# Cross attention: keys turned by a product with a rounded identity, and VectorE takes most copies of turned keys and queries

## The reference, cut to what matters

```python
q = x @ Wq.T + bq                      # 512 x 256, 16 heads of 16
kv = c @ Wkv.T + bkv                   # 1601 x (keys, values)
q = _rms_norm(q, q_gamma)
k = _rms_norm(k, k_gamma)
scores = jnp.einsum('bhnd,bhmd->bhnm', q, k) * scale
attn = jax.nn.softmax(scores, axis=-1)
out = jnp.einsum('bhnm,bhmd->bhnd', attn, v)
```

## Time and profile before

| | us |
|---|---|
| median of 3 runs | 1317.8 |
| lowest and highest | 1315.87, 1321.56 |
| profiled execution, device time | 1319.82 |
| its span, first to last instruction | 1318.1 |
| PE busy | 1209.0 (92%) |
| ACT busy | 907.4 (69%) |
| POOL busy | 706.0 (54%) |
| DVE busy | 659.2 (50%) |

### The profile page before, as it was taken

The page is one execution under the profiler, slowest core; times in us unless marked ns, Lnnn a source line. Parts: engine busy times, 40 slices in busy tenths (PEclk is TensorE's granted clock), DMA queues, the critical chain, the costliest instruction groups (busy, mean ns, idle before and its releaser), DMA issues.

```text
span 1318.1 us, 27754 instructions
## 1 busy us (share of the span) xinstructions
PE 1209.0 (92%) x8712; PEld 739.7 (56%) x8712; DVE 659.2 (50%) x2198; ACT 907.4 (69%) x1824; POOL 706.0 (54%) x810
## 2 busy tenths in 40 slices
PE   5999999999999885799999999999999989999897
PEld 4667766776677573433334333433333278888794
DVE  6666567557655556555035502552555163333336
ACT  4656556646645615667986798679998848888892
POOL 1776557656756701445415540564267757765552
PEclk9999999999999998899999999999999999999999
DMA  7998665445445721001001100101056386666677
GB/s 236 361 318 274 240 206 189 170 153 188 172 149 192 239 64 35 26 13 31 17 1 51 33 17 2 51 2 35 29 208 227 115 302 197 200 219 195 193 270 301
DMA packets 146756, 195.05 MB, mean 148 GB/s; under 512 B 12049, under 2 KB 132513, under 8 KB 145969
## 3 DMA queue, kind: packets, MB, share of 16 engines
q1 hardware_dynamic: 135856, 162.97, 37.9%
q0 software_dynamic: 10752, 30.26, 6.2%
HBM read 71.01 MB, written 122.18 MB: 147 GB/s over the span
## 4 chain that ended last, share of the span: by engine, by line
PE 55%; ACT 16%; issue 10%; DVE 8%; DMA 5%; POOL 3%; SPq 2%; ACTq 0%; DVEq 0%; POOLq 0%
ACT xa_probs L1404 9%; PE sa_pf L354 8%; PE xa_banks L1243 7%; PE xa_banks L1258 6%; PE sa_po L436 5%; PE xa_banks L1126 5%; PE sa_pf L387 4%; PE sa_ps L411 4%; PE mo_banks L2172 4%; PE sa_ptr L422 4%; DMA mo_xs<-rows 3%; ACT sa_probs L478 2%; PE mo_banks L2181 2%; DMA mo_w_all<-in_down_p 1%; PE mo_banks L2160 1%
## 5 line engine op out<-in xcount | busy, mean ns | idle before, releaser
L1404 ACT ACTIVATE xa_probs<-xa_banks 128x1024 f32<-128x1024 f32 (+1 forms) x416 | 401.9, 1045 | 83.2 <-PE xa_banks L1243 82.3
L341 POOL TENSOR_SCALAR sa_probs<-sa_probs,sa_recip 128x128 f32<-128x128 f32 (+3 forms) x256 | 275.7, 1090 | 170.1 <-DVE sa_recip L598 169.6
L478 ACT ACTIVATE sa_probs<-sa_probs,sa_neg_max 128x128 f32<-128x128 f32 (+3 forms) x256 | 141.8, 555 | 155.4 <-DVE sa_neg_max L535 155.3
L1258 PE MATMUL xa_banks<-xa_probs,xa_v_one 128*17 128x512 f32 (+1 forms) x1664 | 218.7, 598 | 6.9 <-ACT xa_q_aug L1350 4.6
L1243 PE MATMUL xa_banks<-xa_q_aug,xa_k_aug 32*128 32x512 f32 (+1 forms) x1664 | 153.3, 442 | 13.5 <-issue 3.4
L2088 POOL DMA_INDIRECT slots<-mo_y,mo_dest x128 | 123.9, 968 | 69.5 <-issue 35.5
L2172 PE MATMUL mo_banks<-mo_xs_t,mo_gu 128*128 128x128 f32 x1024 | 136.3, 276 | 0.0
L2172 PEld LDWEIGHTS mo_banks<-mo_xs_t,mo_gu 128*128 128x128 f32 x1024 | 125.5, 193 | 0.4 <-issue 0.2
L535 DVE CUSTOM_DVE_ANT_0 sa_probs<-sa_ps,sa_toeplitz 128x128 f32<-128x128 f32 (+3 forms) x256 | 115.1, 486 | 14.9 <-PE sa_ps L411 13.4
L1243 PEld LDWEIGHTS xa_banks<-xa_q_aug,xa_k_aug 32*128 32x128 f32 (+1 forms) x1664 | 61.5, 179 | 106.2 <-ACT xa_probs L1404 74.5
L2232 ACT ACTIVATE mo_gu<-mo_w_all 128x512 f32 x128 | 80.7, 630 | 35.3 <-issue 15.3
(11 more groups left out here) (343 smaller groups left out, 2287.5 us busy)
## 6 DMA issues: line engine op xcount, KB each, us to landing
rows<-sa_blank SPq DMA_DIRECT2D x128, 548.0 KB, 3.8
mo_xs<-rows SPq DMA_DIRECT2D x106, 137.0 KB
slots<-sa_blank SPq DMA_DIRECT2D x48, 256.0 KB, 5.0
mo_w_all<-slots SPq DMA_DIRECT2D x22, 512.0 KB, 16.5
xa_raw<-in_ctx_t SPq DMA_DIRECT2D x24, 256.0 KB, 2.8
mo_w_all<-in_gate_up_p SPq DMA_DIRECT2D x2, 2816.0 KB, 16.1
sa_toeplitz<-extended_bias SPq DMA_DIRECT2D x8, 512.0 KB, 7.6
mo_w_all<-in_down_p SPq DMA_DIRECT2D x2, 2048.0 KB, 16.9
```

Of the source, the lines that this page charges most:

```text
L341: pool.tensor_scalar(probs[:, t % SLOTS, 0:w], probs[:, t % SLOTS, 0:w], recip[:, col:col + 1], None, ALU.mult).then_inc(probs_ready, 1)
L478: act.activation(probs[:, t % SLOTS, 0:w], probs[:, t % SLOTS, 0:w], ACT.Exp, bias=neg_max[:, i:i + 1], scale=-1.0, accum_out=sums[:, i:i ...
L1258: last = pe.matmul(banks[32 * i:32 * i + XD + 1, 6 + group % 2, :], v_one[b % 2][0:m, c, 4 * g + i, :], probs[0:m, (2 * j + i // 2) % RING ...
L1404: act.activation(probs[0:m, n % RING, :, :], banks[0:m, 2 * (n % 3):2 * (n % 3) + 2, :], ACT.Exp).then_inc(probs_ready, 1)
```

## The change

Three edits. The four transposes of `turn_k` become four ordinary products in the rounded format, with the keys as weights and a rounded identity as the moving operand (66 instead of 65 columns for the last chunk). GpSimd makes this identity once, early. And a new function `by_scalar` decides who copies a turned part out: ScalarE still does in the prologue and in slots 13, 14 and 16 of each batch; in slots 19, 24 to 29 and 31 to 41 VectorE does it now (the code for that was already in its `evacuate`). The counts on which the waits rest follow. In the diff the last two edits are the first lines of ScalarE's and of VectorE's `evacuate`.

```diff
+    SCALAR_AT = [13, 14, 16]
...
+    def by_scalar(b, s):
+        kind = step_of(b, s)[0]
+        return kind in ("kt", "qt") and (b < 0 or s in SCALAR_AT) or b < 0 and kind in ("x", "kv")
+
...
-            if kind in ("kt", "qt") or b < 0 and kind in ("x", "kv"):
+            if by_scalar(b, s):
                 n_act += 1
             else:
                 n_dve += 1
...
+        ident_r = sb("ident_r", [P, P], F32R)
...
+            chain.then_wait(pool.tensor_copy(ident_r[:], ident[:]))
...
                 for g in range(QUADS):
-                    last = pe.transpose(banks[:, bank, g * P:g * P + m],
-                                        k_tok[(batch * KT + c) % TURNED][0:m, 4 * g:4 * g + 4, :]
-                                        .bitcast(F32).rearrange("p h d -> p (h d)"),
-                                        ident[0:m, 0:m])
+                    last = pe.matmul(banks[:, bank, g * P:g * P + m + m % 2],
+                                     k_tok[(batch * KT + c) % TURNED][0:m, 4 * g:4 * g + 4, :]
+                                     .rearrange("p h d -> p (h d)"),
+                                     ident_r[0:m, 0:m + m % 2], start=True, stop=True)
...
-                if step is None or not (step[0] in ("kt", "qt") or b < 0 and step[0] in ("x", "kv")):
+                if step is None or not by_scalar(b, s):
                     return
...
-                if step is None or step[0] in ("kt", "qt") or b < 0 and step[0] == "x":
+                if step is None or step[0] != "kv" and by_scalar(b, s):
                     return
```

## The result

The changed kernel takes 1330.1 us (median of four runs, 1327.4 to 1331.2) against 1318.0 before: ratio 1.009, 95% interval 1.0073 to 1.0108, so 12 us slower. The forecast was 1325.5, in a range of 1316 to 1331. A second measurement gave 1.0089 (1.0065 to 1.0113).

The account below looks back on a forecast made before the run. PE (92% busy) and ACT were taken as level in cross-attention slots. Batches 0 and 1 +2.4, batch 2 +5.6, prologue -0.3: +7.7 us on 1319.8, 1327.5, so 1325.5 for the median; range 1316 to 1331.

Parts of the forecast that it names:

- The turn: PE's key turns: four products take 0.59 us against 0.58 for transposes; taken as 0, ends -4 and +7 us.
- D: Rival, PE's turns: product not at one pass per column, 0.3 us more per turn, 1337; with other unseen waits 0.06.
- E: Rival, prologue's lone turns: products keep PE's clock up, 1324.3; forecast with C and E together 0.64.
- The 65-key turn: Turn of the 65-key chunk: product 0.56 us against 0.46 for transposes, +0.10 per batch.
- What ACT is relieved of: Copies taken off ACT: worth at most 1.9 us in each of the three batches that prepare a next one.
- only in three places: Per batch, ACT's lateness shows at values products of slots 28 and 41 (0.80, 0.87 late) and slot 38's scores (0.21).
- the walk: VectorE's queue, slots 24 to 30: slot 29's copy late behind part 2, delaying slot 30's turn, +2.08 us per batch.
- part 2: Six VectorE operations of the last RMS group, ahead of slot 29's copy; claimed held by GpSimd's 2.38 us subtraction.
- Rival A: Slot 30: the collision does not happen, only the layer norm's; 1317.8, chance 0.25.
- Batch 2: Slot 38: router's layer norm delays slot 39's copy, PE idle 3.3 us: +2.25, plus +1.3 for a clock fall.
- rival C: Slot 30: the collision brings a clock fall each time, 3 x 1.3 more, 1329.4; forecast with C and E 0.64.
- The prologue's -0.3: Prologue turns on the chain of waits, some at low clock where transposes slow and loads do not: -0.3 us, once.

Follow-up runs that it names:

- turn_only: Changed kernel with the turn by product alone, all copies of turned keys and queries staying on ScalarE: 1318.5 us, ratio 1.0004.
- both_turned: Changed kernel with copies of slot 29, and of slots 39 to 41 in batch 2, on ScalarE, and transposes for products: 1314.3 us, ratio 0.9985.
- both_act: Changed kernel with the copies of slot 29 in each batch and slots 39 to 41 in batch 2 on ScalarE: 1314.9 us, ratio 0.9984.
- few_turned: Changed kernel with transposes, VectorE taking only the copies of slot 27 in three batches and slot 40 in batches 0 and 1: 1313.6 us, ratio 0.9973.
- copy_only: Changed kernel with its copies on VectorE, but the turns still transposes: 1328.9 us, ratio 1.0072.
- ln_act: Changed kernel with the copies of slots 39, 40 and 41 in batch 2 on ScalarE: 1329.0 us, ratio 1.0079.
- ln_again: Changed kernel with the copies of slots 39 to 41 in batch 2 on ScalarE, measured once more: 1329.9 us, ratio 1.0086.
- split_halves: Changed kernel with GpSimd's 2.4 us subtraction of the query split issued as two of half the size: 1332.6 us, ratio 1.0106.
- split_31: Changed kernel with GpSimd's second split of the queries two slots later, in slot 31: 1321.1 us, ratio 1.003.

## Why the prediction was right, and where it was not

**The turn: right, but for the last chunk.** The four products take 0.59 to the scores behind them against 0.58 for the transposes, forecast and measured; turn_only moves the median by 0.4 us. D is out, and so is E: the clock in the prologue's lone turns was lower, not higher. The 65-key turn takes 0.56 to its scores (915.03 to 915.59), as forecast. Its counterpart was misread: the 0.46 of the earlier trace rows is the length of the record, with the end of the last product in it. To the scores the transposes take 0.39 us (timeline of PE, both_turned):

```profile
641.42 0.46 PE L1143 MATMUL xa_banks<-xa_ident,xa_k_tok 65*128 65x65 f32 x4
641.81 0.68 PE L1251 MATMUL xa_banks<-xa_q_aug,xa_k_aug 32*65 32x512 f32 x8
```

So the product costs 0.17 there and not 0.10; in slots 36 to 40 both_turned has -0.34, -0.32 and -0.34 where both_act has -0.16, -0.14 and -0.16.

**What ACT is relieved of: right, the rest of the lateness a little too small.** The late values products came to gaps of 0.28 and 0.21, which by the prediction's own count (0.07 of overlap) are 0.35 and 0.28 late where it had 0.1 to 0.2. few_turned shows that two copies in a batch carry most of the gain. That PE had gaps "only in three places" was also misread: the kernel before has others of 0.6 to 1.05 us in slots 13, 15 and 19, the last by the meeting with GpSimd.

**Slot 30: right, to 0.2 us.** From the scores of slot 24 to the turn of slot 30 17.72 us against 15.82, +1.90 where the walk gave +2.08. In the time frame of before (3.7 added), the subtraction ran 627.32 to 629.72 (walk: 627.3 to 629.75) and the copy of slot 29 630.1 to 630.8 (walk: 630.3 to 631.0). In the walk the third operation of part 2 is the one that is held; in the trace the third starts 0.02 us ahead of the subtraction (623.60 against 623.62) and gets through, and the fourth is held. The end is nearly the same, since either waits for the same subtraction. Rival A's "0.2 us to spare" in the kernel before is misread: from 625.06 to GpSimd's cast at 626.44 it is 1.4 us. That the operation is held for GpSimd's whole instruction rests on four kernels: 2.24 us beside 2.40, 1.15 and 1.20 beside 1.31 and 1.27, 0.17 with nobody beside it, and the copies out of PSUM at 0.68 to 0.69 throughout. The rule quoted from the Trainium skill ("SBUF — State Buffer", Who interferes with whom) agrees. The prediction's "each operation of VectorE that reads SBUF" is too wide: its reductions of 128 x 1024 (L1451) take 1.20 to 1.22 us beside GpSimd and 1.20 to 1.21 with GpSimd idle.

**Batch 2: right.** PE idle for 3.43 us (3.3 forecast); from the turn of slot 37 to the scores of slot 42 14.47 us against 10.68, +3.79 where the steps gave 2.25 + 1.3.

**The term that failed: the clock behind slot 30.** The forecast had "it may come or not, and I leave it out of the sum", and rival C, 1329.4, had it in. It came. Of the 15 stalls of 2.27 to 2.30 us that five records show (the changed kernel twice, copy_only, ln_act and ln_again, each in batches 0 to 2), nine were followed by a fall. Each cost 1.5 to 1.6 us or, where the clock stayed low for longer, 2.9 to 3.2; the mean is 3.7 us for an execution, and C's 3 x 1.3 = 3.9 is nearer than my 0. With split_halves' three (2.24 us by its gap in batch 0; ways longer by 3.2 to 5.0) it is 12 of 18: two of six in batch 0, four in batch 1, all six in batch 2. Why the later ones are surer is open. The kernel before already had such a fall: in its prologue PE was idle for 2.27 us, behind other idle times, and the four transposes of its next key turn took 1.08 us instead of 0.63 (timeline of PE):

```profile
528.47 1.08 PE L1135 MATMUL xa_banks<-xa_ident,xa_k_tok 128*128 128x128 f32 x4 [2.27 <-DVE xa_k_tok L1644]
```

Forecast 1325.5 and 3.7 are 1329.2 against 1330.1 measured. The prediction had the case inside its range, and so the range holds, with 1 us to spare; but it gave the case nothing in the sum and no chance of its own.

**A size in the rest.** The prologue's -0.3 cannot be told: from the first projection to slot 0 before took 61.3 us, the changed kernel 60.3, turn_only 60.2, but copy_only with transposes 60.3 as well. Its reason fails: it had the loads of the product's weights no longer at the low clock, and in the changed kernel's prologue they took 333 ns there instead of 192, and the four products of a turn 1.09 us (526.00) against the 1.08 of transposes above.

## What to carry to other kernels

Before a copy is handed to a less busy engine, walk that engine's queue: what stands ahead of the copy when it falls due, and whether anything there can be held by another engine, decides, not the busy share. Here moving the five copies whose lateness showed as a gap of PE gave all the gain that a median could tell; the other 49 of 54 together cost more than they bought. A stall of the busiest engine is priced with the clock that it may lose behind it, as a chance times 1.5 to 3 us here, not as nothing.

## What the runs showed of the hardware that I had not expected

The fall of TensorE's clock is a matter of chance at 2.27 to 2.30 us of idling (nine of 15; ln_act and ln_again have the same code, and in batch 1 the clock fell in one and not in the other). It came every time behind the layer norm's stall (3.41 to 3.44 us, six of six records that have it). Behind the idle time of slot 13, 0.6 to 1.1 us with other short gaps around it, it was seen twice in 42: behind 1.07 us in ln_again and behind 0.68 in split_31.

In the prologue's last stretch, 530 to 540 us, the granted clock was lower with turns by a product. The Trainium skill ("TensorE: Matmul & The Clock Gate", Part 4: PE-mode transpose), by which transposes do not count as activity in the same way, would have it the other way. The stretch in the kernel before, then in turn_only (busy time and clock):

```profile
530.00:540.00 10.00, 6.57 (x40) 5.42 (x40) 8.87 (x28) 6.70 (x15) 6.11 (x5) 0.80 0.21 55
```

```profile
530.00:540.00 10.00, 8.47 (x42) 7.30 (x41) 7.07 (x26) 5.63 (x11) 3.84 (x4) 0.50 0.22 57
```

All five records of kernels with transposes have 0.80 to 0.84 there, the nine with products 0.50 to 0.75, and three pairs differ in the turn alone: before and turn_only (0.80, 0.50), copy_only and the changed kernel (0.81, 0.66), both_turned and both_act (0.84, 0.50). Slot 0 begins at 536.7 to 541.0, so that this fixed stretch holds some of the first slots in most records. In the ten us that end 1 us ahead of slot 0 it is 0.76 to 0.80 with transposes and 0.50 to 0.55 with products. So the turn's form makes the difference; by what way, its kind, its longer weight loads or the times at which it falls, no run tells apart. It cost nothing that shows, since PE waits for others in that stretch.
